# Two late token tiles are transposed and copied ahead of the bias additions in a one-core mixture-of-experts kernel

## The chip, the cores and the metric

One core of a Trainium2 chip. The metric is the device time of one launch in microseconds (us), median over runs.

## What is computed

1,024 tokens of 512 numbers pass through two blocks. The first (a grouped convolution, then a gated feed-forward net on octonion weights that are quantized to three values) adds its result to `x`. The second mixes channels and sends each token through 2 of 32 experts:

```python
logits = xf @ gate_w.T
w, idx = jax.lax.top_k(logits, TOP_K)            # TOP_K = 2, 32 experts
w = jax.nn.softmax(w, axis=-1)
combine = jnp.zeros((T, NUM_EXPERTS)).at[jnp.arange(T)[:, None], idx].add(w)
def body(acc, params):
    W, b, c = params
    return (acc + c[:, None] * (xf @ W.T + b), None)
out, _ = jax.lax.scan(body, jnp.zeros_like(xf), (expert_w, expert_b, combine.T))
```

Everything is float32. An expert's weights are 1 MB, so 32 MB have to come in.

## The kernel before

**Engines.** Each engine has a list of instructions of its own, written out by hand, and semaphores between them. SP issues the loads, GpSimd (POOL) the gathers and scatters, TensorE (PE) multiplies, VectorE (DVE) and ScalarE (ACT) empty PSUM.

**The expert stage.** Experts are ranked by how many of the first half's tokens chose them. The token-to-expert pairs are cut into 23 tiles of 128 rows (`TILES`, numbered 0 to 22). Tiles 0 to 3 hold two experts each and use only tokens of the first half (here the early tiles). `FIRST` is 4: tiles 4 to 7 are again pairs, of the second half (the late tiles), tile 8 holds four experts, tiles 9 to 16 one each, tiles 17 to 20 (`FIRST_B` is 17) two each, tiles 21 and 22 four each. Tiles 17 to 22 are multiplied in two halves of 256 output columns: all left halves, then all right halves.

**One tile's way.** POOL gathers 128 rows into a `yg` buffer (`gather_tile`, L566). PE transposes them in four matrix instructions into a PSUM bank (`transposes(t)`, L1377): bank 1 for tiles 0 to 3, then bank `t % 2`. DVE copies that bank to `xT[t % 2]` (`xt_evac_tile(t)`, L969). PE multiplies by the expert's weights in `wbuf` in four steps of 128 input rows (`product(t, c0, c1)`, L1405) into bank 2 or 3. ACT scales the result (L759), POOL scatters it to `r_tab` (L574, for half tiles L585), and at the end the rows are read back and added to `acc`. `product(t, ...)` waits for `xt_done`, `transposes(5)` and later ones for the copy of the tile before last, `transposes(4)` for its gather and for `pos_done`. The copy of a tile waits for its transposes and, through `r_mm`, until the product that used its `xT` slot has ended.

**The biases.** `bias(half)` (L1353) makes, with one product for each of four token tiles, the weighted expert biases in banks 5, 6, 7 and 4; DVE's `add_bias(j)` (L941) adds each to `acc`. `bias(1)` uses the same banks and waits for the first four additions (`acc2_done`).

**The weights.** Sixteen `wbuf` buffers. Ranks 0 to 12 are loaded earlier; SP issues ranks 13 to 15 at once after the records, and each load of rank 16 and up (`load_w`, L469) waits until the last tile that uses its buffer has been multiplied (`r_mm`, `released`): rank 16 for the product of tile 4, rank 31 for that of tile 16. One queue on SP carries them in order.

Of the kernel before, what the change touches and what calls it, by code (L numbers as in the profile page):

```python
# [44 lines left out]
NT = TOK // P  # L45
# [9 lines left out]
TPH = NT // 2  # L55
# [3 lines left out]
DC = D // P  # L59
# [19 lines left out]
FIRST = SPLIT // 2  # L79
# [29 lines left out]
def buffer(rank):  # L109

    return rank if rank < NA else SECOND[rank - NA]
# [45 lines left out]
def build_adaln_ffn(nc, a):  # L157
    ctx = ExitStack()
    with ctx:
# [240 lines left out]
        def x_slot(t):  # L400

            return t % 2 if t < FIRST_B else (t - FIRST_B + 1) % 6

        def columns(h):

            return slice(0, D) if h is None else slice(HD * h, HD * (h + 1))

        def in_place(bank_, h):

            return bank_[:] if h is None else bank_[:, 0:HD]  # L410
# [373 lines left out]
        def _(dve):  # L784
# [154 lines left out]
            def add_bias(j):  # L939
                dve.wait_ge(eb_mm, j // TPH + 1)  # L940
                nc.vector.tensor_tensor(acc[:, j], acc[:, j], EBB[j % TPH][:], ALU.add).then_inc(acc2_done, 1)  # L941
# [23 lines left out]
            def xt_evac(i, half_, bank_, used=None):  # L965
                dve.wait_ge(xt_mm, i + 1)
                if used is not None:
                    dve.wait_ge(r_mm, used)
                nc.vector.tensor_copy(xT[half_][:].rearrange("p c t -> p (c t)"), bank_[:]).then_inc(xt_done, 1)  # L969

            def xt_evac_tile(t):

                last = [STEP[s_] + 1 for s_ in STEPS if s_[0] < t and x_slot(s_[0]) == x_slot(t)]
                xt_evac(t, x_slot(t), XT[1 if t < FIRST else t % 2], max(last, default=None))
# [10 lines left out]
            for half in range(2):  # L985
# [56 lines left out]
                for t in range(TPH):  # L1042
                    j = half * TPH + t
# [16 lines left out]
            place(NT - 1)  # L1060
            for t in range(2, FIRST):
                xt_evac_tile(t)
            for half in range(2):
                for j in range(TPH):
                    add_bias(TPH * half + j)
                for t in range(FIRST + 2 * half, FIRST + 2 * half + 2):
                    xt_evac_tile(t)

            dve.wait_ge(cnt_mm, 1)
            link(nc.vector.scalar_tensor_tensor(junk[0:E], BY[0:E, 0:E], 1.0, ident[0:E, 0:E], ALU.mult, ALU.mult, accum_out=cnt))  # L1070
# [62 lines left out]
        def _(pe):  # L1133
# [213 lines left out]
            def bias(half):  # L1347

                if half == 1:
                    pe.wait_ge(acc2_done, TPH)  # L1350
                for q in range(TPH):
                    rows_ = slice(E * q, E * (q + 1))
                    v = mm(EBB[q][:], combT[rows_, half], eb[rows_], start=True, stop=True)  # L1353
                v.then_inc(eb_mm, 1)
# [19 lines left out]
            def across(t, n, b, half_, bank_):  # L1374
                pe.wait_ge(yg_in[b], n * 16)
                for c in range(DC):
                    v = nc.tensor.transpose(bank_[:, P * c:P * (c + 1)], yg[b][:, P * c:P * (c + 1)], ident)  # L1377
                v.then_inc(xt_mm, 1)

            def transposes(t):  # L1380

                if t == 0:
                    pe.wait_ge(silu_done, 2 * HC)
                elif t < FIRST:
                    pe.wait_ge(xt_done, t)
                elif t == FIRST:
                    pe.wait_ge(pos_done, NT)
                else:
                    pe.wait_ge(xt_done, t - 1)
                across(t, t // U + 1, t % U, t % 2, XT[1 if t < FIRST else t % 2])  # L1390

            def product(t, c0, c1, h=None):

                n = STEP[t, h]
                if c0 == 0:
                    pe.wait_ge(xt_done, t + 1)
                    if n >= 2:
                        pe.wait_ge(res_done, n - 1)
                    if t < 2:
                        pe.wait_ge(h_done, 2 * HC)  # L1400
                    for _, _, r, _ in TILES[t]:
                        pe.wait_ge(w_in[buffer(r)], 16 if r < NA else 32)
                for c in range(c0, c1):
                    for p0, w, r, _ in TILES[t]:
                        v = mm(in_place(RS[n % 2], h)[p0:p0 + w], xT[x_slot(t)][:, c, p0:p0 + w], wbuf[buffer(r)][:, c, columns(h)], start=(c == 0), stop=(c == DC - 1))  # L1405
                if c1 == DC:
                    v.then_inc(r_mm, 1)
# [76 lines left out]
            product(2, 0, 2)  # L1484
            transposes(3)
            product(2, 2, DC)
            product(3, 0, DC)
            pe.wait_ge(eb_in, 16)
            pe.wait_ge(combt_done, 2)
            bias(0)  # L1490
            transposes(FIRST)
            transposes(FIRST + 1)
            product(FIRST, 0, DC)
            bias(1)
# [157 lines left out]
```

## Time and profile before

| | |
|---|---|
| median of 3 runs | 304.82 us (304.78 to 306.13) |
| the profiled execution, its own time | 301.33 us |
| its span | 299.5 us |
| mean granted TensorE clock | 0.969 of full speed |
| busy: PE / DVE / POOL / ACT | 269.5 / 130.3 / 80.9 / 78.7 us |
| the chain that ended last | PE 78%, DMA 11%, DVE 3% |
| moved by DMA | 58.12 MB, 194 GB/s on average |

A page of the profile lists groups of instructions by line; the trace behind it gives them in order of time, and for each what its engine had waited for. The profiled execution is 3.49 us shorter than the median, so sums are made against its own time and carried over as differences.

### The profile page before, as it was taken

The numbers are of one execution on the slowest core, as the hardware profiler recorded it, in microseconds if no ns is written. First come the engines' busy times: TensorE is split into PE (matmuls) and PEld (weight loads), VectorE is DVE, ScalarE is ACT, GpSimd is POOL, SyncE is SP. The second block draws the span as 40 slices with busy tenths as digits, with TensorE's granted clock in tenths as the row PEclk, the third lists the DMA queues.
The fourth block names the chain that finished last, engine by engine and source line by source line (L and its number), as shares of the span: only waits on it lengthen the run. The fifth ranks groups of instructions, "written<-read, shape, count | busy, mean of one in ns | idle before, by whom it ended". The sixth has DMA issues, their size and how long they took to land.

```text
span 299.5 us, 4493 instructions
## 1 busy us (share of the span) xinstructions
PE 269.5 (90%) x1600; PEld 170.4 (57%) x1600; DVE 130.3 (43%) x378; ACT 78.7 (26%) x144; POOL 80.9 (27%) x81
## 2 busy tenths in 40 slices
PE   7877999999999999999999999979999999969500
PEld 3245677688777878788877743323344444636200
DVE  3368766767523423574414554044443111200536
ACT  2456664143111142333211122101011111112100
POOL 1423400000000000046142233574544554334600
PEclk9999999999999999999999999979999999999955
DMA  7990000000000100191199990499999999822977
GB/s 267 396 327 1 3 0 1 2 2 0 0 35 35 38 35 2 15 368 39 38 372 415 420 410 20 132 316 382 349 343 351 421 421 410 335 117 93 333 253 265
DMA packets 21462, 58.12 MB, mean 194 GB/s; under 512 B 4361, under 2 KB 12207, under 8 KB 17088
## 3 DMA queue, kind: packets, MB, share of 16 engines
q1 hardware_dynamic: 15776, 47.89, 42.0%
q0 software_dynamic: 4288, 8.43, 8.1%
q10 hardware_dynamic: 1376, 1.51, 1.5%
q8 instruction: 13, 0.21, 0.3%
q14 instruction: 9, 0.07, 0.1%
HBM read 51.23 MB, written 10.85 MB: 207 GB/s over the span
## 4 chain that ended last, share of the span: by engine, by line
PE 78%; DMA 11%; DVE 3%; issue 2%; POOL 2%; ACT 2%; SPq 1%; POOLq 0%; ACTq 0%; DVEq 0%
PE bank L1259 26%; PE bank L1405 22%; PE bank L1441 14%; DMA wbuf<-in_w 5%; PE bank L1314 3%; PE bank L1377 3%; DMA xp_first<-in_xp 2%; PE bank L1142 2%; PE bank L1335 2%; DMA wbuf<-r_tab 2%; POOL r_tab L585 2%; DMA r_tab<-res,row_halves 2%; PE bank L1321 1%; PE bank L1204 1%; DVE y0lo L830 1%
## 5 line engine op out<-in xcount | busy, mean ns | idle before, releaser
L1405 PE MATMUL bank<-wbuf,xT 128*64 128x512 f32 (+4 forms) x480 | 86.6, 491 | 4.9 <-DMA wbuf<-in_w 2.9
L1405 PEld LDWEIGHTS bank<-wbuf,xT 128*64 128x64 f32 (+2 forms) x480 | 34.0, 136 | 41.3 <-issue 33.0
L558 POOL DMA_INDIRECT slots<-kept,sid x16 | 15.8, 990 | 123.8 <-DVE sid L936 120.7
L1441 PE MATMUL bank<-md,hid 128*128 128x512 f32 x176 | 48.2, 414 | 0.0
L759 ACT ACTIVATE res<-bank,recs 128x512 f32<-128x512 f32 (+1 forms) x29 | 17.4, 599 | 83.3 <-PE bank L1405 83.3
L1441 PEld LDWEIGHTS bank<-md,hid 128*128 128x128 f32 x176 | 31.8, 189 | 8.3 <-issue 2.9
L969 DVE COPY xT<-bank 128x512 f32<-128x512 f32 x23 | 15.8, 690 | 46.8 <-PE bank L1377 46.8
L1259 PE MATMUL bank<-y0hi,mg 128*128 128x512 f32 x88 | 35.3, 412 | 0.6 <-ACT y0hi L641 0.6
L1259 PE MATMUL bank<-y0hi,mu 128*128 128x512 f32 x88 | 33.7, 396 | 0.7 <-DVE mu L834 0.7
L1259 PE MATMUL bank<-y0lo,mg 128*128 128x512 f32 x88 | 33.7, 394 | 0.2 <-DVE y0lo L830 0.2
L1259 PE MATMUL bank<-y0lo,mu 128*128 128x512 f32 x88 | 33.6, 393 | 0.0
L891 DVE TENSOR_TENSOR htmp<-bank,stmp 128x512 f32<-128x512 f32 x22 | 15.2, 692 | 31.3 <-PE bank L1259 20.6
L566 POOL DMA_INDIRECT yg<-y_tab,recs x23 | 23.4, 1017 | 16.4 <-DMA recs<-slots 9.9
L574 POOL DMA_INDIRECT r_tab<-res,recs x17 | 17.3, 1018 | 26.0 <-ACT res L759 24.8
L687 ACT ACTIVATE hid<-htmp 128x512 fp32r<-128x512 f32 x22 | 13.9, 630 | 23.3 <-DVE htmp L891 23.3
L683 ACT ACTIVATE stmp<-bank,small 128x512 f32<-128x512 f32 x22 | 15.2, 690 | 16.4 <-PE bank L1259 16.3
L1259 PEld LDWEIGHTS bank<-y0hi,mg 128*128 128x128 f32 x88 | 16.4, 188 | 5.2 <-issue 1.9
L1259 PEld LDWEIGHTS bank<-y0hi,mu 128*128 128x128 f32 x88 | 16.5, 188 | 4.7 <-ACT mu L656 1.1
L1259 PEld LDWEIGHTS bank<-y0lo,mg 128*128 128x128 f32 x88 | 16.4, 188 | 3.9 <-DVE y0lo L830 0.7
L1259 PEld LDWEIGHTS bank<-y0lo,mu 128*128 128x128 f32 x88 | 16.4, 188 | 3.3
L1377 PEld LDWEIGHTS bank<-cf,yg 128*128 128x128 f32 x92 | 10.4, 140 | 13.3 <-issue 13.2
L901 DVE SCALAR_TENSOR_TENSOR acc<-bank,small,acc 128x512 f32<-128x512 f32 x8 | 6.0, 751 | 26.3 <-PE bank L1441 26.3
(186 smaller groups left out, 273.0 us busy)
## 6 DMA issues: line engine op xcount, KB each, us to landing
wbuf<-in_w SPq DMA_DIRECT2D x32, 1024.0 KB, 9.3
wbuf<-r_tab SPq DMA_DIRECT2D x8, 512.0 KB, 5.9
acc<-in_x SPq DMA_DIRECT2D x1, 2048.0 KB, 15.0
y_tab<-yv SPq DMA_DIRECT2D x8, 256.0 KB, 3.6
base<-in_base SPq DMA_DIRECT2D x3, 352.0 KB, 7.5
xp_first<-in_xp SPq DMA_DIRECT2D x1, 1040.0 KB, 7.3
xp_second<-in_xp SPq DMA_DIRECT2D x1, 1040.0 KB, 9.6
out<-acc SPq DMA_DIRECT2D x4, 256.0 KB, 3.4
```

Source lines behind the costliest of these rows:

```text
L558: pool.indirect_dma_start(out=slots, out_offset=bass.IndirectOffsetOnAxis(ap=sid[:, j, k:k + 1], axis=0), in_=rec[:, j, k], in_offset=None ...
L566: pool.indirect_dma_start(out=yg[b][:], out_offset=None, in_=y_tab[0:HALF] if first else y_tab, in_offset=bass.IndirectOffsetOnAxis(ap=rec ...
L574: pool.indirect_dma_start(out=r_tab, out_offset=bass.IndirectOffsetOnAxis(ap=recs[:, slot, 1:2].bitcast(U32), axis=0), in_=res[b][:], in_o ...
L683: nc.scalar.activation(stmp[:, n % 2], G[n % 2][:], ACT.Silu, scale=wsc[:, 0:1]).then_inc(silu_done, 1)
L687: nc.scalar.activation(hid[:, :, 0, n % HC], tiles_of(htmp[:, n % 2]), ACT.Copy).then_inc(hhi_done, 1)
L759: nc.scalar.activation(res[b][:, columns(h)], in_place(bank_, h), ACT.Copy, scale=recs[:, slot, 2:3].bitcast(F32)).then_inc(res_done, 1)
L891: nc.vector.tensor_tensor(htmp[:, n % 2], UU[n % 2][:], stmp[:, n % 2], ALU.mult).then_inc(h_done, 1)
L969: nc.vector.tensor_copy(xT[half_][:].rearrange("p c t -> p (c t)"), bank_[:]).then_inc(xt_done, 1)
L1259: v = mm(bank_[:], tab[:, r, n % HC], (y0hi, y0lo)[part][:, r, HALF * half:HALF * (half + 1)], start=(r == 0 and part == 0), stop=(r == R ...
L1377: v = nc.tensor.transpose(bank_[:, P * c:P * (c + 1)], yg[b][:, P * c:P * (c + 1)], ident)
L1405: v = mm(in_place(RS[n % 2], h)[p0:p0 + w], xT[x_slot(t)][:, c, p0:p0 + w], wbuf[buffer(r)][:, c, columns(h)], start=(c == 0), stop=(c == ...
L1441: v = mm(DN[j % 2][:], hid[:, t, part, c], md[:, c], start=(c == 0 and part == 0), stop=(c == HC - 1 and part == 1))
```

## The change

Two lists change. On PE the four transposes of tile 4 stand ahead of the last quarter of tile 3's product, where they stood behind `bias(0)`. On DVE the copies of tiles 4 and 5 stand ahead of the first four bias additions instead of behind them, and the copy of tile 6 ahead of the second four.

```diff
@@ -1060,11 +1060,14 @@
             for t in range(2, FIRST):
                 xt_evac_tile(t)
-            for half in range(2):
-                for j in range(TPH):
-                    add_bias(TPH * half + j)
-                for t in range(FIRST + 2 * half, FIRST + 2 * half + 2):
-                    xt_evac_tile(t)
+            xt_evac_tile(FIRST)
+            xt_evac_tile(FIRST + 1)
+            for j in range(TPH):
+                add_bias(j)
+            xt_evac_tile(FIRST + 2)
+            for j in range(TPH, NT):
+                add_bias(j)
+            xt_evac_tile(FIRST + 3)
@@ -1484,11 +1487,12 @@
             transposes(3)
             product(2, 2, DC)
-            product(3, 0, DC)
+            product(3, 0, DC - 1)
+            transposes(FIRST)
+            product(3, DC - 1, DC)
             pe.wait_ge(eb_in, 16)
             pe.wait_ge(combt_done, 2)
             bias(0)
-            transposes(FIRST)
             transposes(FIRST + 1)
             product(FIRST, 0, DC)
             bias(1)
```

PE before, from the third quarter of tile 3's product to the first of tile 4's (`yg4` holds tile 4's rows, bank 5 is the first of `bias(0)`):

```order
L1405 MATMUL bank3<-wbuf3_86,xT1_97 64x512
L1405 MATMUL bank3<-wbuf7_90,xT1_97 64x512
L1353 MATMUL bank5<-eb_131,combT_58 128x512 [waits combt_done,eb_in]
L1353 MATMUL bank6<-eb_131,combT_58 128x512
L1353 MATMUL bank7<-eb_131,combT_58 128x512
L1353 MATMUL bank4<-eb_131,combT_58 128x512
L1377 MATMUL bank0<-cf_129,yg4_119 128x128 [waits yg_in4,pos_done]
L1377 MATMUL bank0<-cf_129,yg4_119 128x128 x3
L1377 MATMUL bank1<-cf_129,yg5_120 128x128 [waits yg_in5,xt_done]
L1377 MATMUL bank1<-cf_129,yg5_120 128x128 x3
L1405 MATMUL bank2<-wbuf0_83,xT0_96 64x512 [waits w_in0,w_in4,res_done,xt_done]
```

PE with the change, the same place (lines have moved by three):

```order
L1380 MATMUL bank0<-cf_129,yg4_119 128x128 [waits yg_in4,pos_done]
L1380 MATMUL bank0<-cf_129,yg4_119 128x128 x3
L1408 MATMUL bank3<-wbuf3_86,xT1_97 64x512
L1408 MATMUL bank3<-wbuf7_90,xT1_97 64x512
L1356 MATMUL bank5<-eb_131,combT_58 128x512 [waits combt_done,eb_in]
L1356 MATMUL bank6<-eb_131,combT_58 128x512
L1356 MATMUL bank7<-eb_131,combT_58 128x512
L1356 MATMUL bank4<-eb_131,combT_58 128x512
L1380 MATMUL bank1<-cf_129,yg5_120 128x128 [waits yg_in5,xt_done]
L1380 MATMUL bank1<-cf_129,yg5_120 128x128 x3
L1408 MATMUL bank2<-wbuf0_83,xT0_96 64x512 [waits w_in0,w_in4,res_done,xt_done]
```

The transposes of tile 4, with their wait for the gather, now come ahead of the two last matrix products of tile 3.

DVE before, after the copies of tiles 2 and 3:

```order
L941 TENSOR_TENSOR acc_55<-acc_55,bank5 128x512 [waits eb_mm]
L941 TENSOR_TENSOR acc_55<-acc_55,bank6 128x512 [waits eb_mm]
L941 TENSOR_TENSOR acc_55<-acc_55,bank7 128x512 [waits eb_mm]
L941 TENSOR_TENSOR acc_55<-acc_55,bank4 128x512 [waits eb_mm]
L969 COPY xT0_96<-bank0 128x512 [waits r_mm,xt_mm]
L969 COPY xT1_97<-bank1 128x512 [waits r_mm,xt_mm]
```

With the change the two `COPY` rows, with the same waits, stand ahead of these four additions.

## Rows read from the trace of the kernel before

**Rows 1.** The chain that ended last: start, length in us, engine, tile, line
```profile
188.64 5.30 PE bank L1405 x24
193.94 1.11 PE bank L1353 x8
...
195.69 1.88 DVE acc L941 x3
197.56 0.61 DVE xT L969
...
198.22 5.35 PE bank L1405 x16
...
205.23 3.58 PE bank L1405 x16
...
253.64 14.80 DMA wbuf<-in_w
```
**Rows 2.** PE in order of time: start, length, line, tiles, [idle before <-releaser]
```profile
193.87 1.14 PE L1353 MATMUL bank<-eb,combT 32*128 32x512 f32 x8
194.94 1.30 PE L1377 MATMUL bank<-cf,yg 128*128 128x128 f32 x8
198.22 5.35 PE L1405 MATMUL bank<-wbuf,xT 128*64 128x512 f32 x16 [1.98 <-DVE xT L969]
203.50 1.14 PE L1353 MATMUL bank<-eb,combT 32*128 32x512 f32 x8
204.57 0.66 PE L1377 MATMUL bank<-cf,yg 128*128 128x128 f32 x4
```
**Rows 3.** DVE in order of time, the first additions and the copies of tiles 4, 5
```profile
195.08 2.48 DVE L941 TENSOR_TENSOR acc<-acc,bank 128x512 f32<-128x512 f32 x4 [5.71 <-PE bank L1353]
197.48 1.28 DVE L969 COPY xT<-bank 128x512 f32<-128x512 f32 x2
```
**Rows 4.** Stretches: us, busy of PE, PEld, DVE, ACT, POOL; PEclk, DMA share, GB/s
```profile
198.50:199.00 0.50, 0.50 (x4) 0.14 (x2) 0.26 (x1) 0.00 (x0) 0.50 (x1) 1.00 0.98 385
199.00:199.50 0.50, 0.50 (x4) 0.24 (x2) 0.00 (x0) 0.00 (x0) 0.42 (x1) 0.53 1.01 418
202.00:202.50 0.50, 0.50 (x2) 0.02 (x2) 0.00 (x0) 0.00 (x0) 0.19 (x2) 0.55 1.06 434
```
**Rows 5.** Line 566 from 190 to 191 us: the gather of tile 4
```profile
L566 POOL DMA_INDIRECT yg<-y_tab,recs x1: 1048/1048/1048, 190.5 to 190.5; - x1
...
DMA to landing us min/median/max: 3.3/3.3/3.3
```
**Rows 6.** Line 469: the load of rank 16 (203 to 204 us)
```profile
L469 SPq DMA_DIRECT2D wbuf<-in_w x1: 333/333/333, 203.8 to 203.8; - x1
...
DMA to landing us min/median/max: 8.9/8.9/8.9
```
**Rows 7.** Stretches, columns as in rows 4
```profile
210.00:215.00 5.00, 5.00 (x26) 1.77 (x24) 2.93 (x18) 0.69 (x1) 2.15 (x3) 1.00 0.93 374
215.00:220.00 5.00, 5.00 (x38) 1.80 (x38) 1.28 (x5) 0.69 (x1) 2.87 (x3) 1.00 0.96 328
220.00:225.00 5.00, 5.00 (x40) 2.18 (x29) 2.35 (x13) 0.69 (x1) 2.40 (x4) 1.00 0.90 335
225.00:230.00 5.00, 5.00 (x16) 2.30 (x15) 1.30 (x5) 0.69 (x1) 2.51 (x3) 1.00 0.95 344
240.00:245.00 5.00, 5.00 (x16) 2.41 (x15) 0.69 (x1) 0.69 (x1) 2.87 (x4) 1.00 1.02 422
260.00:265.00 5.00, 3.72 (x32) 2.04 (x26) 1.38 (x2) 0.95 (x2) 2.03 (x3) 1.00 0.51 210
265.00:270.00 5.00, 3.36 (x60) 2.23 (x64) 0.00 (x0) 0.47 (x1) 1.38 (x2) 1.00 0.16 65
```
**Rows 8.** PE in order of time, the products of tiles 21 and 22
```profile
265.80 1.93 PE L1405 MATMUL bank<-wbuf,xT 128*32 128x256 f32 x32 [2.08 <-DMA wbuf<-in_w]
268.58 12.58 PE L1405 MATMUL bank<-wbuf,xT 128*32 128x256 f32 x160 [0.85 <-DMA wbuf<-in_w]
```

## The prediction

> **What bounds the kernel now.** I read the chain that ended last first. PE holds it through the expert stage with one gap near the change: after `bias(0)` the chain leaves PE for DVE's bias additions and one copy, and returns at 198.22 us [rows 1]. The second thing to see there is its end: from 253.64 to 268.44 the chain is one DMA, the load of rank 31, for 14.80 us. So the stage around the change belongs to PE and DVE, and the stage that follows ends in a transfer. What is gained in the first reaches the end only through the second.
>
> Then PE in order of time. The transposes of tiles 4 and 5 end at 194.94 + 1.30 = 196.24, and PE then stands idle 1.98 us for a copy of DVE [rows 2]. DVE shows why: it begins the four additions at 195.08, when tile 4's rows are not yet transposed, and the copy PE needs waits behind them until 197.48 [rows 3].
>
> Then the clock. Product 4 took 5.35 us; product 5, of the same 16 instructions, 3.58 [rows 1]. The granted clock shows the difference: full (2.4 GHz) until 199, half (1.2 GHz) from there to past 202 [rows 4], right behind the idle time. The gap thus costs its 1.98 us and, later, 5.35 - 3.58 = 1.77 us more.
>
> **The change, part by part.**
>
> *Transposes of tile 4 into product 3.* No instruction is added; four transposes move from behind `bias(0)` to ahead of the last quarter of product 3. They issue no DMA and pass no queue. Their length is about 0.59 us, by the 0.66 us of the single group in [rows 2] less its overlap. What is new is where their wait stands. Product 3 ends at 188.64 + 5.30 = 193.94; its last quarter is 3.58/4 = 0.90 us, so PE comes to the transposes at 193.04. The gather of tile 4 is issued at 190.5 and lands 3.3 us later, at 193.8 [rows 5]. PE would stand about 0.85 us, to 193.9, with the last quarter, `bias(0)` and the transposes of tile 5 queued behind. Then 0.59 (transposes, to 194.5), 0.90 (last quarter, 195.4), 1.11 (`bias(0)` by [rows 1], 196.5), 0.59 (tile 5, 197.1).
>
> *Copies of tiles 4 and 5 first.* DVE can copy tile 4 at 194.5, when product 2 has long freed the slot, and is done by 195.2, at 0.61 to 0.69 us a copy. Product 4 then starts when PE arrives, at 197.1, where it started at 198.22: 1.1 us earlier. The copy of tile 5 waits for its transposes and for product 3, runs from 197.1 to 197.8, and only then come the additions that were ready at 196.5: 2.48 us [rows 3], to 200.3. `bias(1)` waits for these four. Product 4 covers them if it takes 3.58 us, to 200.7, by 0.4 us. If that cover is missing, PE waits for the difference only.
>
> *The clock.* PE's idle time of 1.98 us goes and one of 0.85 us comes. No row shows what 0.85 us does. The nearest: idle times of 1.98 us with a fall behind it [rows 2, 4], and of 2.08 us at 263.7 with the clock full from 260 to 270 [rows 7, 8]. 0.85 us is shorter than both, and the 0.85 us at 267.7 [rows 8] is the nearest of all; I take no fall, so 1.77 us are won. The other end is a fall as before: nothing won.
>
> *Copy of tile 6 ahead of the second additions.* It waits for transposes that stand behind `bias(1)`, at about 202.4; the additions then end at 205.6, ahead of the wait in front of the count of tokens, which PE reaches behind product 5 at about 206.6. Nothing won or lost; the cover is product 5, and without it at most one copy, 0.7 us.
>
> *Sum at the end of product 4:* 198.22 + 5.35 = 203.57 becomes 197.1 + 3.58 = 200.7, so **2.9 us**. From there PE has no wait for 50 us, and everything that hangs on it, the loads included, is issued 2.9 us earlier.
>
> *What the loads make of it.* Rank 16, issued at 203.8, landed 8.9 us later [rows 6]; rank 31 took 14.80 us [rows 1]. A load of 1 MB at the 422 GB/s of a well-filled stretch [rows 7] needs 2.5 us, so the last one spent most of its time behind others. Issuing it earlier may only lengthen its queue. Lower bound of the gain: nothing, since the engines' share is near 1 from 205 to 255 us. Upper bound: all 2.9. Between them: from 210 to 230 us the stretches moved 374, 328, 335 and 344 GB/s, mean 345, against 422 later [rows 7]. In 20 us that is 6.9 MB, which at 422 would take 16.4 us; 3.6 us lie there as idle time and slow packets. Their idle part alone, by the shares 0.93, 0.96, 0.90, 0.95, is 0.07 + 0.04 + 0.10 + 0.05 = 0.26 of 5 us, 1.3 us. Loads that are issued earlier keep the engines supplied, which takes the idle part away for sure and the slow part perhaps. I take **1.4 us**, nearer the part that is read as idle, and keep 0 and 2.9 for the range.
>
> The Trainium skill, "DMA: Bandwidth & Descriptors", section "Queues, rings and completion order", says that each DMA engine takes the work of one ring in order. By it rank 16, issued 2.9 us earlier, would stand behind ranks 13 to 15 and start when they end, so its own 2.9 us would be lost in the queue; the long landing of rank 31 agrees.
>
> *The tail.* PE now waits 2.08 us for rank 30 and 0.85 us for rank 31 [rows 8]. If the loads come 1.4 us earlier and PE 2.9, the first wait grows to 2.08 + 1.5 = 3.6 us. The clock could fall there. Half clock over the 1.93 us of product 21 costs 1.93 us, of which the 0.85 us wait behind it hides 0.85; I take no fall and keep +1.1.
>
> **Sum.** -1.4 us on 301.33 gives 299.9 for the profiled execution. The median is 304.82, 3.49 above it; the same difference gives **303.4 us**. A measurement of this kernel can tell about 0.5%, 1.5 us, from no change.
>
> **The rivals.**
>
> *All of it arrives.* For it: the missing 3.6 us in [rows 7] are more than the 2.9; the chain runs through PE until 253.64 and only then into the load. Against: the slow rate continues from 225 to 230, when several loads are queued, so part of it isn't lack of work. 304.82 - 2.9 = 301.9 us.
>
> *Nothing arrives.* The time is set by the DMA engines with most to do, which are never without work from 200 us on. In the last stretch the mean share is 0.51 [rows 7] while PE still waits: some engines are done and others not. An engine with a backlog gains nothing from more of it. 304.8 us. The Trainium skill, "Perfetto Trace Analysis", section "What 'DMA-bound' means", counts being bound on specific DMA engines as a case of its own; by that rule the sum would be 0 instead of -1.4.
>
> *The clock falls at the tail (slower).* If nothing arrives at the loads, PE's wait for rank 30 is 2.08 + 2.9 = 4.9 us. The fall near 199 lasted from about 199 to 202.4 [rows 4]. If one of twice that length, 6.8 us, begins as PE resumes, 3.4 us of work are lost, less the 0.85 us wait that hides some: +2.5 us, 307.4. It decides if the loads have not moved and the clock falls at the longer wait. Against it: the wait of 2.08 us left the clock full to 270 us [rows 7], and a fall that begins within the wait is partly spent in it.
>
> *The gather comes late (slower).* The wait for tile 4's rows now holds PE directly. In the profile it costs 0.85 us; from 193.8 + 1.1 = 194.9 on product 4 starts no earlier than before, and each further us costs one, where DVE's additions used to hide it. A landing 2.6 us later, with the clock falling behind the longer wait, gives +1.5 us, 306.3. Against: records and gather depend on nothing that the change moves.
>
> *The change doesn't do what it says:* the order of both lists shows that it does; I give this nothing.
>
> **How the numbers follow.** Forecast (the loads gain 0.7 to 2.1 us) 0.36; all arrives 0.28; nothing, or up to 1.1 more at the tail, 0.18; clock at the tail 0.10; late gather 0.08. Over 1.5 us faster: 0.28 and a quarter to a third of the forecast, 0.11: 0.39. Over 1.5 us slower: the last two, 0.18. The rest, 0.43, is within 0.5%. The range runs from all arriving with a little more (301.3) to the late gather (306.2); the tail's clock case and the worst of the late gather stay outside. The likeliest case's own range is 302.7 to 304.1.
>
> **What would show it.** Right: PE idle near 193 for under 1 us, on the gather; the idle time at 196 gone; product 4 at 3.6 us; clock full from 190 to 210; rank 16's load issued near 200.9 but landing about 11 us later; a rate above 345 GB/s from 207 to 227; PE's wait for rank 30 at 3 to 4 us. Wrong: product 4 still at half clock; the wait within product 3 over 2 us; PE's waits at the tail unchanged (all arrived), or rank 31 landing at 268 as before (nothing arrived).

## The result and the profile after

The change does not gain. Its median is 305.72 us (303.70 to 310.26, 20 runs) against 303.11 us for the kernel before, run beside it (298.85 to 306.69, 20 runs): a ratio of 1.0173, 95% interval 1.0137 to 1.0208. Medians here and below are over all runs, while each ratio compares only the fast runs, those within 1.5% of the fastest of their own kernel (18 of 20 for the change here, about half of the 20 for the kernel before), so it isn't the quotient of the two medians, which is 1.0086 here. The forecast was 1.4 us faster. In three later sessions on known chips the ratio came out smaller, down to 0.9986; that spread became the main question. A run given below without a ratio is one execution, except e4.

The profiled execution took 303.70 us (span 301.9 us), the shortest of the 20. TensorE (PE) in order of time, columns as in [rows 2]:

```profile
194.14 0.63 PE L1380 MATMUL bank<-cf,yg 128*128 128x128 f32 x4 [1.12 <-DMA yg<-y_tab,recs]
194.70 1.08 PE L1408 MATMUL bank<-wbuf,xT 128*64 128x512 f32 x4
195.71 1.14 PE L1356 MATMUL bank<-eb,combT 32*128 32x512 f32 x8
196.78 0.66 PE L1380 MATMUL bank<-cf,yg 128*128 128x128 f32 x4
197.37 3.65 PE L1408 MATMUL bank<-wbuf,xT 128*64 128x512 f32 x16
206.14 2.09 PE L1356 MATMUL bank<-eb,combT 32*128 32x512 f32 x8 [5.12 <-DVE acc L941]
208.16 1.11 PE L1380 MATMUL bank<-cf,yg 128*128 128x128 f32 x4
209.21 3.65 PE L1408 MATMUL bank<-wbuf,xT 128*64 128x512 f32 x16
```

The first five rows are what was forecast, to 0.3 us. PE waits 1.12 us for tile 4's gather inside product 3; the 1.98 us of [rows 2] are gone; product 4 begins at 197.37 and takes 3.65 us, where it began at 198.22 and took 5.35. It ends at 201.0, 2.5 us earlier than before. Then PE stands for 5.12 us ahead of `bias(1)`. Product 5 begins at 209.21, against 205.23 in [rows 1]. VectorE (DVE) and ScalarE (ACT) show what it waited for:

```profile
194.81 0.69 DVE L969 COPY xT<-bank 128x512 f32<-128x512 f32 x1 [5.50 <-issue]
203.01 0.69 DVE L969 COPY xT<-bank 128x512 f32<-128x512 f32 x1 [7.50 <-remote]
203.62 2.47 DVE L941 TENSOR_TENSOR acc<-acc,bank 128x512 f32<-128x512 f32 x4
...
205.31 0.69 ACT L759 ACTIVATE res<-bank,recs 128x512 f32<-128x512 f32 x1 [8.73 <-remote]
```

The copy at 203.01 is tile 5's. Its transposes ended at 196.78 + 0.66 = 197.44 and product 3, which used its slot, at 195.8; the forecast had it at 197.1. So DVE stood 5.6 us after everything was there. The four additions of `bias(0)` queue behind it, and `bias(1)` waits for them. ACT is late in the same way: it scales product 4's rows at 205.31, though that product ended at 201.0. "remote" means that the profile finds nothing in this core's records that released the instruction. The signals (semaphore increments) that PE sends on finishing came late to those waiting for them. That both engines themselves were held up instead is unlikely: SP's load of rank 16 waits for the same product 4, and SP took it up at 205.3 us, in the same tenth of a microsecond as ACT its row; and PE went on at 206.14, as soon as DVE's additions had ended. Starts are recorded, but the ends of matrix instructions are modelled, so whether PE finished late or its signal travelled late can't be told.

SyncE (SP) was slow in the same stretch. Line 469 is the load of a rank; columns: engine, operation, count, then shortest/median/longest in ns, first and last start in us:

```profile
L469 SPq FUSED_REGOPS  x32: 3/37/447, 125.5 to 257.6; - x32
L469 SPq MOVE wbuf<-in_w x32: 2/29/708, 125.6 to 257.6; - x32
L469 SPq DMA_DIRECT2D wbuf<-in_w x32: 3/333/691, 125.7 to 257.7; - x32
```

A register move that takes 29 ns in the median took 708 ns once, and an issue 691 instead of 333. Both of these lie between 195 and 201 us, in the loads of ranks 13 to 15. The shortest entries, 2 and 3 ns, are as strange, since the same steps take 29 and 333 ns in the median: either the steps or the times recorded for them were disturbed.

The clock, columns as in [rows 4]:

```profile
198.00:202.00 4.00, 3.02 (x16) 0.72 (x10) 0.00 (x0) 0.00 (x0) 3.08 (x4) 1.00 0.99 345
202.00:206.00 4.00, 0.00 (x0) 0.00 (x0) 2.99 (x5) 0.69 (x1) 1.23 (x2) 0.97 1.00 401
206.00:210.00 4.00, 3.86 (x16) 1.57 (x18) 0.77 (x3) 0.00 (x0) 2.04 (x2) 0.60 0.98 383
210.00:230.00 20.00, 20.00 (x122) 7.74 (x119) 9.96 (x43) 2.75 (x4) 8.20 (x8) 1.00 0.82 274
```

The fall is not gone; it has moved behind the new idle time, to `bias(1)` (2.09 us instead of 1.14) and the transposes of tile 6. Loads of rank 16 and up start later, so 210 to 230 us carried 274 GB/s, where the four rows of [rows 7] average 345. The end, in the chain that ended last and in PE's order of time:

```profile
195.85 7.13 another core or an unknown queue
...
257.69 13.97 DMA wbuf<-in_w
```
```profile
269.00 1.93 PE L1408 MATMUL bank<-wbuf,xT 128*32 128x256 f32 x32 [1.23 <-DMA wbuf<-in_w]
271.80 12.58 PE L1408 MATMUL bank<-wbuf,xT 128*32 128x256 f32 x160 [0.86 <-DMA wbuf<-in_w]
```

The chain holds 7.13 us, to 202.98, without an instruction of the core: the wait for the late signal. Rank 31's load took 13.97 us, nearly the 14.80 of [rows 1], and simply began 4 us later; product 22 starts 3.2 us later than in [rows 8].

### The profile page after: what moved, and what is told of

Same layout as the page of the kernel before. It is cut to its first block, busy times and chain, and to the rows that moved or that the text cites. A ratio compares the mean times of both kernels' runs of the same rounds, so it can differ in the third digit from the quotient of the medians.

```text
span 301.9 us, 4493 instructions
## 1 busy us (share of the span) xinstructions
PE 269.4 (89%) x1600; PEld 170.3 (56%) x1600; DVE 130.2 (43%) x378; ACT 78.7 (26%) x144; POOL 81.2 (27%) x81
## 4 chain that ended last, share of the span: by engine, by line
PE 71%; DMA 12%; issue 6%; DVE 4%; another core or an unknown queue 2%; ACT 2%; POOL 2%; SPq 1%; POOLq 0%; ACTq 0%; DVEq 0%
PE bank L1262 26%; PE bank L1408 16%; PE bank L1444 14%; DMA wbuf<-in_w 5%; PE bank L1317 3%; PE bank L1380 2%; DMA xp_first<-in_xp 2%; PE bank L1145 2%; DMA wbuf<-r_tab 2%; PE bank L1338 2%; POOL r_tab L585 2%; DMA r_tab<-res,row_halves 1%; PE bank L1324 1%; DMA yg<-y_tab,recs 1%
## 5 line engine op out<-in xcount | busy, mean ns | idle before, releaser
L1408 PE MATMUL bank<-wbuf,xT 128*64 128x512 f32 (+4 forms) x480 | 85.2, 483 | 2.1 <-DMA wbuf<-in_w 2.1
```

## The experiments

The theory that came to be called C: PE's signals between about 195 and 203 us come late in some executions, whatever the order of the lists, and the change hangs more on them. D, for the last three runs, adds that the change gains where they are in time. Each expectation says what its rivals suppose. A copy or addition is called late by the time from the end of the PE instructions it waits for to its start, where nothing of its own engine is in the way.

### The change again, and its parts

e1_change is the change unaltered. e2_dve_only takes only DVE's half of the diff, e3_pe_only only PE's. e4_behind3 keeps DVE's half and stands tile 4's transposes behind all of product 3, still ahead of `bias(0)`:

```diff
-            product(3, 0, DC - 1)
-            transposes(FIRST)
-            product(3, DC - 1, DC)
+            product(3, 0, DC)
+            transposes(FIRST)
```

> The change itself again, beside the others. Theory A (late signal): in the profile of the change VectorE's copy of tile 5 began at 203.0 us, 5.6 us after the transposes it waits for stand in the record (197.4), the additions behind it ended at 206.1 and TensorE stood 5.1 us before the second bias products; if that is what the change brings, a second profile shows the same hole, within 2 us, and the ratio to before is 1.01 to 1.02. Theory B (a disturbance of one profiled execution): the copy of tile 5 begins within 0.3 us of its transposes, and the wait before the second bias products is under 1 us; the ratio may still be 1.01 to 1.02, and then has another cause.

> VectorE's new order alone, TensorE as before. The transposes of tile 4 end near 195.6 us, product 4 starts near 196.4 instead of 198.2 and its clock does not fall: stage gain 1.8 + 1.8 = 3.6 us at the end of product 4. Theory A, if it hangs on VectorE's order (copy of tile 5 ahead of the additions, so that a late signal of its transposes holds up the additions and with them the second bias products): a hole of 4 to 6 us before the second bias products, ratio 1.01 to 1.02. If it hangs on TensorE's order alone: no hole, ratio 0.985 to 1.0.

> TensorE's new order alone, the additions ahead of both copies as before. TensorE waits about 1 us inside product 3 and then about 2 us for the copy of tile 4, behind the four additions that start near 197: product 4 starts near 200.3, 2 us later than before, and the clock falls as before. If TensorE's order is the cause of the loss: ratio 1.007 to 1.02, with the late signal of the transposes of tile 5 seen here too. If VectorE's order is: ratio 1.0 to 1.007.

> The change with the transposes of tile 4 behind all of product 3 (ahead of the first bias products) instead of inside it. The gather of tile 4 has landed then, so TensorE's 1.1 us wait inside product 3 goes. If the wait inside product 3 matters for the loss (TensorE's sequencer held there, and the code refill that stood at 190.5 us before coming at 195.8 us): ratio under 1.0, refill back near 190. If only VectorE's order does: ratio 1.01 to 1.02 as the change.

Measured, with the kernel before at 302.34 us (23 runs): the change 302.16 us, ratio 1.0051 (0.9998 to 1.0105); DVE's part 301.14 us, 0.9966 (0.9905 to 1.0027); PE's part 304.64 us (6 runs), 1.0111 (1.0027 to 1.0194); transposes behind product 3, 304.46 us (6 runs, no ratio). The profile of PE's part alone:

```profile
193.88 0.63 PE L1377 MATMUL bank<-cf,yg 128*128 128x128 f32 x4 [1.06 <-DMA yg<-y_tab,recs]
194.43 1.08 PE L1405 MATMUL bank<-wbuf,xT 128*64 128x512 f32 x4
195.44 1.14 PE L1353 MATMUL bank<-eb,combT 32*128 32x512 f32 x8
196.51 0.66 PE L1377 MATMUL bank<-cf,yg 128*128 128x128 f32 x4
203.02 5.24 PE L1405 MATMUL bank<-wbuf,xT 128*64 128x512 f32 x16 [5.85 <-issue]
```

All four profiles have a late signal somewhere. In e1 the copy of tile 5 was 3.3 us late and PE idled 2.88 us ahead of `bias(1)`; in e2 the copy of tile 4 was 3.8 us late, PE idled 3.87 us ahead of product 4 at half clock; in e3 the additions of `bias(0)` were 3.3 us late; in e4 the copy of tile 5 was 5.7 us late, and PE idled 5.27. What is delayed is whichever signal falls into the stretch. In e4 PE stood only 0.19 us ahead of tile 4's transposes, and nothing got better: taking that wait away isn't enough. Of the expectations, that for e3 held (1.007 to 1.02, if PE's order is the cause). Theory A's for e1 didn't: its ratio is below 1.01 and its idle time 2.2 us shorter than in the first profile. Nor did that of 4 to 6 us ahead of `bias(1)` for e2, where PE stood ahead of product 4 instead and the ratio lies in the other case's 0.985 to 1.0.

### The kernel before, profiled twice more

If the lateness belongs to the change, the kernel before must be free of it. e5 and e6 are the kernel before, e7 the change, one run each.

> The kernel before, profiled anew. In the one profile of it every signal of TensorE came within 0.1 us; in the profiles of the change and of its three variants signals of TensorE that fall between 195 and 203 us came 3 to 6 us late, and SP's register steps for the loads of ranks 13 to 15 took 0.7 us instead of 0.04. Theory A (the change's orders bring this about): here again all signals within 0.1 us, SP's three loads 1.1 us apart, product 4 begins near 198.2 us. Theory C (every version has it in most executions, and the profile of before that I predicted from was one without): the first additions begin 3 to 5 us behind the first bias products, or product 4 begins at 200 us or later, and the time is 302 to 306 us instead of 301.3.

> The kernel before once more, the same expectations: one undisturbed profile could be luck either way. Theory A: undisturbed again. Theory C: at least one of the two is disturbed.

> The change a third time, profiled beside the two of before. Theory A and C: signals late again. A third possibility, that lateness is random in both: undisturbed, product 4 begins at 197.1 and ends at 200.7, the second bias products follow within 0.5 us, and rank 16's load is issued near 200.9.

306.06, 304.48 and 305.92 us. PE ahead of product 4 and of product 5, in e5 and in e7:

```profile
202.68 6.45 PE L1405 MATMUL bank<-wbuf,xT 128*64 128x512 f32 x16 [6.18 <-DVE xT L969]
...
210.71 3.65 PE L1405 MATMUL bank<-wbuf,xT 128*64 128x512 f32 x16
```
```profile
207.54 2.09 PE L1356 MATMUL bank<-eb,combT 32*128 32x512 f32 x8 [6.59 <-DVE acc L941]
...
210.60 4.05 PE L1408 MATMUL bank<-wbuf,xT 128*64 128x512 f32 x16
```

The kernel before has it too: 6.18 us of idle time where [rows 2] has 1.98, and product 5 at 210.71, as late as the change's 210.60. In e6 it was 3.70 us and product 5 came at about 207.5. What was late there: the copy of tile 5 in e5 started 9.0 us after its transposes had ended, in e6 7.2 us. The execution on which the prediction rests was one of the undisturbed ones.

### One copy ahead instead of two

e8 keeps PE's half, but only tile 4's copy goes ahead of the additions, so that `bias(1)` hangs on `bias(0)` alone; tile 6's copy goes back behind the second four:

```diff
             xt_evac_tile(FIRST)
-            xt_evac_tile(FIRST + 1)
             for j in range(TPH):
                 add_bias(j)
-            xt_evac_tile(FIRST + 2)
+            xt_evac_tile(FIRST + 1)
             for j in range(TPH, NT):
                 add_bias(j)
-            xt_evac_tile(FIRST + 3)
+            for t in range(FIRST + 2, FIRST + 4):
+                xt_evac_tile(t)
```

> The change, but with only tile 4's copy ahead of the first four additions; tile 5's copy stands behind them, and tile 6's behind the second four, as before. Theory C: TensorE's signals between 195 and 203 us come 3 to 6 us late in most executions of every version, and the change loses at the second bias products what it gains at product 4, because the additions stand behind a copy that waits for the late signal of tile 5's transposes. Then the additions here start with the signal of the first bias products (199 to 201 us in three profiles of the change), the second bias products start at 201.5 to 203.5 instead of 203.6 to 207.5, and the ratio to before is 0.985 to 0.998. Rival D: the stage ends when the late signals end, whatever the order; then product 5 starts at 206 to 210 as in the change and the ratio is 1.0 to 1.01.

301.48 us against 301.25: ratio 1.0048 (1.0004 to 1.0092). The additions, now ahead of tile 5's copy, were late themselves (200.46, when `bias(0)` ended at 196.3), and PE idled 2.57 us. `bias(1)` came at 202.99, as theory C had it, but the ratio is rival D's, 1.0 to 1.01. Another order meets another late signal.

### The loads of ranks 13 to 15 moved ahead

In the disturbed profiles SP is slow while it issues these loads. e9 issues them before SP's wait for the records, near 178 us, in the kernel before; e10 does so in e8; e11 in the change.

```diff
+            for r in range(13, NA):
+                load_w(r)
             sp.wait_ge(recs_out, 2 * NT * 16)
             for g in range(1, len(RECS)):
                 load_recs(g)
-            for r in range(13, E):
+            for r in range(NA, E):
                 load_w(r)
```

> Before, with SP's loads of ranks 13 to 15 issued ahead of its wait for the records (near 178 us instead of 195). Theory E: the late signals come from the weight loads, the small record loads and the gathers meeting at 195 to 203 us; with the loads gone from there the signals come within 0.3 us, SP's steps take 0.04 us, product 4 starts at 198 and the ratio is 0.96 to 0.985 (also since the loads have a start of up to 7 us on the tail). Rival F: lateness belongs to the records and gathers, or to the code refills near 195, and not to these loads: signals late as before, product 4 at 200 or later, ratio 0.98 to 1.0. A loss (up to 1.01) if the loads hold up the record stores at 178 to 187 us and with them the gather of tile 4.

> Both together: TensorE's order of the change, one copy ahead of the additions, the early loads. If the two gains are separate (order: 0 to 1.5%, loads: 1 to 4%), ratio 0.95 to 0.98. If the late signals were all that the order could save from and the loads take them away: the same as the early loads alone within 0.5%.

> The change with the early loads, one look. If the signals come in time then, my sum for the stage can be tested as it stood: product 4 starts 197.1 us or, with the gather later, up to 198; ends 3.6 us later; the second bias products follow within 0.5 us; clock full throughout; against the early loads without the change the end of product 4 is 2 to 3 us earlier.

304.42 us, ratio 1.0074 (1.0025 to 1.0123); 302.16, 1.0071 (1.0030 to 1.0112); 300.23 us (one run). In all three the signals from 194 to 203 us were in time, to 0.4 us. Nothing was won: the 3 MB delayed the records, whose loads began at 189.88 us in e9 and at 186.68 in e8 on the same chip, 3.2 us later, and PE waited for the gather in e9

```profile
196.56 1.08 PE L1379 MATMUL bank<-cf,yg 128*128 128x128 f32 x4 [2.07 <-DMA yg<-y_tab,recs]
198.37 1.09 PE L1379 MATMUL bank<-cf,yg 128*128 128x128 f32 x4 [0.72 <-issue]
199.39 5.62 PE L1407 MATMUL bank<-wbuf,xT 128*64 128x512 f32 x16
```

and 3.98 and 3.65 us in the other two. The lateness was not gone either; it had moved to 205 to 208 us. DVE's second additions and ACT's row of product 4 in e10:

```profile
208.17 2.48 DVE L943 TENSOR_TENSOR acc<-acc,bank 128x512 f32<-128x512 f32 x4 [3.79 <-remote]
```
```profile
208.13 0.69 ACT L761 ACTIVATE res<-bank,recs 128x512 f32<-128x512 f32 x1 [7.67 <-remote]
```

`bias(1)` had ended at 206.45 and product 4 at 205.38, so these are 1.7 and 2.7 us late; in e9 the additions were 1.6 us late, in e11 ACT 2.6. No clean profile has that. At that point the loads looked like the cause of the lateness, but a cause that moved with the records and the gathers, 3 us later, fits as well (rival F in part).

### The same loads held back, and the change on a fourth chip

e12 (the kernel before) and e13 (the change) hold them until tile 4 has been multiplied; e14 is the change, e15 DVE's part alone, both timed.

```diff
+            sp.wait_ge(r_mm, FIRST + 1)
             for r in range(13, E):
                 load_w(r)
```

> The kernel before, with the loads of ranks 13 to 15 issued only when tile 4 has been multiplied (near 203 us) instead of at 195. Theory C (PE's signals between 195 and 203 us come late while those 3 MB come in): the first additions begin within 0.5 us of the end of bias(0), the copy of tile 4 within 0.5 us behind them, PE's idle time ahead of product 4 is 2 us as in the rows of before; a signal that is late, if any, is late behind 204 us. Rival (the lateness has nothing to do with these loads): copy or additions come 3 to 5 us late again and PE idles 3.7 to 6 us. The time is of no interest here: 8 us without loads cost 2 to 6 us at the end.

> The change, with the loads of ranks 13 to 15 issued only when tile 4 has been multiplied. Theory C: the copy of tile 5 follows its transposes within 0.5 us, the additions end near 200.5, bias(1) follows product 4 with under 0.5 us of idle time, product 5 begins near 202.5 as my prediction had it. Rival: the copy of tile 5 is late by 3 us or more and PE idles over 2.5 us ahead of bias(1).

> The change once more, on another chip, beside the DVE order alone. Theory C (each of the change's two places lies in the stretch of late signals): ratio to before 1.003 to 1.015, over that of the DVE order alone; product 3's wait about 1 us. Rival (what the first timing showed is the change's own cost, the same everywhere): ratio near 1.017.

> DVE's order alone once more, on the same chip as the change. If the cost lies in PE's wait inside product 3: ratio 0.995 to 1.003, below the change's by 0.5 to 1.2%. Rival (it is the order of DVE's copies that costs): ratio equal to the change's.

Held back: 305.04 and 304.37 us (6.3 and 6.7 us above the medians of the kernel before and of the change on this chip, as the late loads cost at the end), all signals in time. But on this chip they were in time with the loads in their usual place as well, so e12 and e13 show nothing of the loads' part. The useful result is e14, the change without disturbance: 297.72 us (296.79 to 299.26, 12 runs) against 298.74 (296.21 to 301.51, 23 runs), ratio 0.9986 (0.9953 to 1.0018). Its PE, then DVE, then line 469:

```profile
194.04 0.63 PE L1380 MATMUL bank<-cf,yg 128*128 128x128 f32 x4 [1.16 <-DMA yg<-y_tab,recs]
194.60 1.08 PE L1408 MATMUL bank<-wbuf,xT 128*64 128x512 f32 x4
195.61 1.14 PE L1356 MATMUL bank<-eb,combT 32*128 32x512 f32 x8
196.68 0.66 PE L1380 MATMUL bank<-cf,yg 128*128 128x128 f32 x4
197.27 3.65 PE L1408 MATMUL bank<-wbuf,xT 128*64 128x512 f32 x16
200.85 1.14 PE L1356 MATMUL bank<-eb,combT 32*128 32x512 f32 x8
201.92 0.66 PE L1380 MATMUL bank<-cf,yg 128*128 128x128 f32 x4
202.51 3.65 PE L1408 MATMUL bank<-wbuf,xT 128*64 128x512 f32 x16
```
```profile
197.37 0.69 DVE L969 COPY xT<-bank 128x512 f32<-128x512 f32 x1 [1.97 <-PE bank L1380]
197.98 2.47 DVE L941 TENSOR_TENSOR acc<-acc,bank 128x512 f32<-128x512 f32 x4
```
```profile
...
L469 SPq MOVE wbuf<-in_w x32: 29/29/38, 125.5 to 250.9; - x32
L469 SPq DMA_DIRECT2D wbuf<-in_w x32: 332/333/362, 125.5 to 251.0; - x32
```

This is the stage of the prediction row by row: product 4 at 197.27 (forecast 197.1), the additions done at 200.45 (200.3), product 4 done at 200.9 (200.7), `bias(1)` without a wait, product 5 at 202.51, 2.7 us earlier than in [rows 1]. The clock is full throughout this stage. And SP's register steps are short in every load. The end:

```profile
250.99 14.41 DMA wbuf<-in_w
```
```profile
262.54 1.93 PE L1408 MATMUL bank<-wbuf,xT 128*32 128x256 f32 x32 [1.47 <-DMA wbuf<-in_w]
265.53 12.58 PE L1408 MATMUL bank<-wbuf,xT 128*32 128x256 f32 x160 [1.05 <-DMA wbuf<-in_w]
```

Product 22 starts 3.05 us earlier than in [rows 8], and the execution took 297.69 us, 3.64 less than the profiled one before. Against that profile everything arrived. The two profiles are of different chips, though. Against the runs of before on the same chip, by medians, 1.0 us arrived, and the interval of the ratio includes 1, so no gain is shown. The ratios expected for e14, 1.003 to 1.015 by theory C and 1.017 by its rival, were both missed: the theory had supposed late signals on every chip.

e15: 297.74 us, ratio 0.9984 (0.9947 to 1.0021), equal to the change; its profile has product 4 at 196.38, full clock and no wait in this stage. At the tail it fared worse: PE waited 2.22 us for rank 30, the granted clock was 0.79 on average from 265 to 270 us, and product 21 took 2.40 us, the rest 13.53, where [rows 8] has 1.93 and 12.58. That profile's own time is 299.88, 2.1 us above the median of e15.

### Before, the change and PE's part on a fifth chip

No edit but PE's half of the diff in e18.

> The kernel before, unchanged, timed against itself. It prices what a ratio of this measurement is worth and gives a profile of before beside that of the change on one chip. All theories: ratio 0.997 to 1.003. If it comes out over 1.004 or under 0.996, ratios near 1.005 of the earlier runs say nothing. Its profile: with signals in time (as in e12 to e15) product 4 near 198.2 behind 1.98 us of idle time, product 5 near 205.2; with late signals PE idles 3.7 to 6 us ahead of product 4.

> The change again on the chip of e16. Theory D (the change wins about 2.7 us at product 5 where PE's signals come in time, and nothing where they come late; the loads at the end pass on only a part): signals in time: product 5 near 202.5, ratio 0.994 to 1.000, PE's two waits for ranks 30 and 31 longer together than before's by what is lost; signals late: product 5 at 206 to 211, ratio 1.000 to 1.012. Rival (the ratio has nothing to do with the late signals): ratio outside these bounds for the state that its profile shows.

> PE's order alone, on the same chip. DVE still adds before it copies, so the copy of tile 4 waits for bias(0), which stands 1 us later than before. Signals in time: product 4 near 199.5 behind about 2 us of idle time with the clock falling behind it, product 5 near 206.5, 1.3 us later than before; ratio 1.000 to 1.008. Signals late: ratio 1.004 to 1.018, as in e3. Rival (PE's part costs nothing): ratio within 0.003 of that of e16.

The kernel before against itself: 1.0007 (0.9958 to 1.0056), so a ratio of 1.005 with such an interval is at the edge of what is told apart. The change: 304.19 against 300.24 us, ratio 1.0061 (0.9996 to 1.0126); the quotient of the medians, 1.013, is larger. PE's part: 304.91 us, 1.0108 (1.0037 to 1.0179), the same as on the first chip. All three profiles are disturbed. DVE in e16, then PE in e16, e17 and e18:

```profile
195.05 2.48 DVE L941 TENSOR_TENSOR acc<-acc,bank 128x512 f32<-128x512 f32 x4 [5.74 <-PE bank L1353]
199.32 0.69 DVE L969 COPY xT<-bank 128x512 f32<-128x512 f32 x1 [1.79 <-remote]
```
```profile
200.07 5.32 PE L1405 MATMUL bank<-wbuf,xT 128*64 128x512 f32 x16 [3.78 <-DVE xT L969]
...
206.97 3.65 PE L1405 MATMUL bank<-wbuf,xT 128*64 128x512 f32 x16
```
```profile
205.33 1.69 PE L1356 MATMUL bank<-eb,combT 32*128 32x512 f32 x8 [4.44 <-DVE acc L941]
...
208.00 4.23 PE L1408 MATMUL bank<-wbuf,xT 128*64 128x512 f32 x16
```
```profile
201.72 5.35 PE L1405 MATMUL bank<-wbuf,xT 128*64 128x512 f32 x16 [4.23 <-DVE xT L969]
...
208.66 3.65 PE L1405 MATMUL bank<-wbuf,xT 128*64 128x512 f32 x16
```

Here lies a difference between the orders, in these three profiles. The kernel before sends the signal of `bias(0)` at about 195, and DVE's additions began at once, at 195.05. PE's part sends it 1.9 us later, because of its wait for the gather (0.94 us) and the transposes ahead of it, and the additions began only at 198.59; product 5 came 1.7 us later. The change hangs `bias(1)` on the signal of tile 5's transposes, sent at 197.3, in the middle of the stretch. Product 5 came 1.0 us later than before's. It isn't a rule, however: in e5 and e6, the kernel before as well, the additions of `bias(0)` were themselves 3.0 and 1.0 us late. And e18's loss has a part that needs no late signal: its expectation puts product 5 1.3 us later with all signals in time, since DVE's additions, and tile 4's copy behind them, wait for a later `bias(0)`.

## Why the prediction was wrong

It said 303.4 us, 0.5% faster, with most chance on faster or the same. The first session was 1.7% slower; over four sessions the change stood at 1.0173, 1.0051, 0.9986 and 1.0061 (by quotients of medians 1.0086, 0.9994, 0.9966 and 1.0132). That 305.72 us lies near the 306.3 of the late-gather rival is chance, since the gather was in time. The base had moved too: the kernel before, 304.82 us by 3 runs, stood at 303.11 by 20.

**Transposes inside product 3, and the wait for the gather: right.** 0.85 us forecast; 1.12 measured, and 0.90, 1.16, 1.16 and 1.02 in the other runs of the change. Product 4 began at 197.0 to 197.4 in all five. The late-gather rival decides from 194.9 us on; the rows were there by 194.1, so it wasn't reached.

**The clock: right where it was asked.** Waits of 0.9 to 1.2 us inside product 3 left product 4 at full clock in every profile of the change. The 1.77 us were won there, and in the four disturbed profiles of the change 1.4 to 1.8 us were paid back at half clock behind the next idle time.

**Copies first, then the additions: the step that failed.** The text has the copy of tile 5 run "from 197.1 to 197.8" and the additions end at 200.3, so that product 4 covers them "by 0.4 us". In e14 that is exact to 0.3 us, so the sum holds for an undisturbed execution. In the first profile, e1, e7 and e17 the copy began at 203.01, 200.45, 204.40 and 202.20, and PE idled 5.12, 2.88, 6.59 and 4.44 us. The text did say what would follow if the cover were missing, but not what could take it away: a signal that comes 3 to 7 us after the work it reports. That has no row in the profile of before. The sum was made on one execution, 3.49 us below the median of its own kernel; the step "the same difference gives 303.4" supposed that what made the other executions longer was the same for both orders. At least part of it sat in the very stretch that the change rearranges: in e5 and e6, the kernel before, product 5 came 5.5 and 2.3 us later than in [rows 1] and the executions took 4.7 and 3.2 us longer. e16 shows that it isn't the whole of it: product 5 1.7 us later, but only 0.45 us longer in all.

**Second additions behind tile 6's copy: right,** nothing lost in e14.

**What the loads pass on: mis-sized.** 1.4 of 2.9 us was taken. From the start of product 5 to that of product 22 it is 63.35 us in the profile before, 63.02 in e14, 62.59 in the first profile, 62.72 in e16 and 63.90 in e17. The whole shift arrives, gain or loss, to within about 0.8 us in these five; e18, with 62.03 us, and e8, with 65.05 (its product 5 ran partly at half clock, and PE waited 2.75 us for rank 30), lie further out. Rank 31's load took 14.80, 14.41, 13.97, 14.10 and 14.70 us, and 13.41 (e18) to 15.47 (e8) in the other profiles with these loads in their usual place where the chain shows it alone; e15, the earliest to issue it (250.10 us), took 14.94. So little was lost in the queue: e14 issued it 2.65 us earlier than the profile before and it landed 3.04 earlier; e15 against e18, the widest pair, 7.04 and 5.51 us. The two sentences from the Trainium skill ("DMA: Bandwidth & Descriptors", section "Queues, rings and completion order", and "Perfetto Trace Analysis", section "What 'DMA-bound' means") were read as lowering this term; taking work in order was no loss, since every load moved together.

**The tail:** no fall of the clock there in these profiles, as forecast; rank 30's wait was 1.23 and 1.47 us, not 3 to 4. The rival wasn't empty: in e6, e8 and e15, behind waits of 2.33, 2.75 and 2.22 us, the clock did fall, and the last 192 instructions of PE in [rows 8] took 1.6, 1.5 and 1.4 us longer.

Which part costs is shown only for one: PE's part alone cost 1.1% in both sessions, each with an interval above 1 (0.8 and 1.6% by medians). DVE's part alone stands at 0.997 and 0.998, each with 1 inside. PE's part adds no instruction; what differs is that PE reaches the end of `bias(0)` 1.9 us later. That this delay accounts for the 1.1% is argued, not shown. No version was shown to beat the kernel before.

**What stays open.** What makes the signals late. With ranks 13 to 15 in their usual place, 12 of 15 profiles are disturbed, on four chips that are known and in the first session, and 3 are not, two of them on one chip. With these loads moved ahead, on a chip that showed the lateness in e8, the stretch to 203 us was clean three times of three, but signals were late at 205 to 208 us instead; moving the loads also moved the records and the gathers, and which of them the lateness follows is not told apart.

Code refills (the profile's instruction queue, 16 KB each) don't decide it: the one nearest to this stretch came at 190.5 us in the profile before and at 195.7 to 200.0 in e12 to e15, all clean, and at 190.4 in e16, which is disturbed.

Part of it may be the recording itself: the disturbed traces hold 2,908 to 3,032 semaphore events (e9 to e11 among them) and the clean ones 3,505 to 3,517, of the same 4,493 instructions. The missing ones go with the lateness in time: from 190 to 200 us the clean traces hold 267 to 290 events and the disturbed ones 63 to 105; in e9 to e11 it is 134 to 177 there, and 36 to 46 from 200 to 210 us, where the clean ones have 108 to 162. But events are missing from 130 to 150 us too (114 to 139 against 252 to 255), and nothing is behind afterwards: the record loads begin between 186.7 and 187.4 us in the clean profiles and the disturbed ones alike (e9 to e11 apart). The Trainium skill, "NOTIFIC — Programmer's Manual", section "When the ring fills", has one setting in which records that don't fit are lost and one in which the producer is held; lost records are what these counts look like, and that an engine was held is not shown by any run here.

Against recording alone: the runs whose profile wasn't kept differ in the same direction, medians of the kernel before being 302.34, 301.25 and 300.24 us on three chips with disturbed profiles and 298.74 on the clean one; and the kept profiles of the change lie at the medians of their runs (302.04 against 302.16 us, 304.03 against 304.19, 297.69 against 297.72). The record has a span and a granted clock for the other runs too, so it doesn't show that they ran without any recording. For it: on the chip of e5 to e7 the one other run of the kernel before took 297.59 us, the two profiled ones 304.48 and 306.06.

Open too is why the first session gave 1.017, or 1.009 by medians, and how the kernel before reaches 296.21 us in its best runs, 5 us below its own clean profile.

## What to carry to other kernels

Before summing on one profile, compare its time with the median: where they differ by more than the gain hoped for, take a second profile, and look at whether the difference lies in the stretch to be changed. An order in which a long list waits behind one freshly sent signal is fragile, and a cover of 0.4 us is none where signals can come 3 us late. Whether putting first what depends on the oldest signal cures it is not shown; e8 tried it for `bias(1)` and was no faster than the kernel before. Here a shift of PE's work that precedes every later load arrived at the last product nearly whole, though the last transfer took 14 us from issue to landing.

## What the runs showed of the hardware

- By the profile's times, a signal from PE can reach DVE, ACT and SP several us after the instruction it reports, in the profiles of the change 3 to 7 us: a copy at 203.01 whose transposes ended at 197.44, a scaling at 205.31 behind a product that ended at 201.0. Nothing else on those engines stood ahead of either. The longest of all, 9.0 us, is tile 5's copy in e5.
- In the same stretches SP's register move took up to 722 ns (e5) instead of 29, an issue up to 1,396 (e7) instead of 333, and other such steps were recorded with 2 or 3 ns; in e7 the issue is that of rank 13.
- Whether it happens goes with the chip or the session: four profiles of four clean on one chip, eleven of eleven disturbed from 195 to 203 us on four others with the loads in their usual place. In three more there, with the loads moved ahead, signals were late from 205 to 208 us.
- TensorE's clock: one idle time of 1.16 us ahead of product 4's stage had no fall behind it (e14). Two in a row, 0.75 and 1.24 us, did (e12): product 4 took 5.29 us. Ahead of product 21 a wait of 2.19 us had none (e2: 1.93 us) and one of 2.22 us did (e15: 2.40 us).
- With 3 MB of weight loads issued from 177.6 us on (e9), the small record loads began 3.2 us later than in e8.
